# Cross-attention of a six-layer decoder kernel: context held once in float32 on four row groups, and scores computed twice

## The reference

```
q = layernorm(x).reshape(N, Q, 16, 16);  k = v = ctx.reshape(N, 375, 16, 16)
energy = einsum('nqhd,nkhd->nhqk', q, k)
energy = where(mask == 0, -1e20, energy)
attn   = softmax(energy / sqrt(256), axis=-1)
out    = einsum('nhqk,nkhd->nqhd', attn, v).reshape(N, Q, 256)
x      = x + out @ W_out.T
```

## Time and profile before

| | |
|---|---|
| median of three runs | 1690.42 us |
| the profiled execution | 1694.06 us |
| its span, first to last instruction | 1692.0 us |
| granted TensorE clock, mean | 0.942 |
| busy: TensorE, VectorE, ScalarE, GpSimd | 91%, 50%, 43%, 28% |
| phase A ends with VectorE's residual of its last batch | 360.1 us |
| phase B ends with its last residual | 685.5 us |

### The profile page before, as it was taken

How to read it: one execution, slowest core, us unless ns; L and a number is a source line. 1 busy time by engine, 2 the same in 40 slices (tenths; PEclk the granted TensorE clock), 3 DMA queues, 4 the chain that set the end, 5 groups by cost and what they waited for, 6 DMA issues and landing times.

```text
span 1692.0 us, 32657 instructions
## 1 busy us (share of the span) xinstructions
PE 1534.2 (91%) x10944; PEld 1093.8 (65%) x10944; DVE 840.0 (50%) x1896; ACT 731.2 (43%) x2003; POOL 480.1 (28%) x535
## 2 busy tenths in 40 slices
PE   5999999979888898599997999999989998899995
PEld 5888888857777787255554475656566665566553
DVE  2555555546666685355553121111136664566665
ACT  1111121126676686266664323122226664454552
POOL 1111111121111120598884000000023332455541
PEclk8999999977898898799998999999999999899995
DMA  8152221148797989000000100000000000000001
GB/s 202 48 93 65 64 62 55 55 72 102 105 108 92 107 101 207 1 1 0 0 1 1 47 1 1 0 0 0 0 6 1 0 0 1 9 9 11 8 4 44
DMA packets 58226, 71.10 MB, mean 42 GB/s; under 512 B 9552, under 2 KB 54848, under 8 KB 58160
## 3 DMA queue, kind: packets, MB, share of 16 engines
q1 hardware_dynamic: 58160, 70.23, 23.7%
HBM read 56.07 MB, written 14.15 MB: 41 GB/s over the span
## 4 chain that ended last, share of the span: by engine, by line
PE 76%; DVE 7%; DMA 6%; issue 4%; ACT 3%; POOL 2%; SPq 2%; DVEq 0%; ACTq 0%; POOLq 0%
PE banks L287 42%; PE banks L661 6%; DMA b_cp<-mask_scratch 5%; PE banks L280 4%; PE banks L566 3%; PE banks L597 3%; PE banks L674 3%; PE banks L687 3%; PE banks L587 2%; PE banks L613 2%; PE banks L538 2%; PE banks L664 2%; DVE area L1403 1%; PE banks L644 1%; DMA room<-in_bo 1%
## 5 line engine op out<-in xcount | busy, mean ns | idle before, releaser
L1109 ACT ACTIVATE area<-banks,area 112x112 f32<-112x112 f32 x768 | 208.9, 361 | 145.5 <-DVE area L1403 134.0
L661 PE MATMUL banks<-area 128*112 128x448 f32 x384 | 178.6, 547 | 7.7 <-ACT area L1109 3.9
L1349 DVE TENSOR_REDUCE area<-banks 112x2 f32<-112x750 f32 x128 | 119.9, 937 | 98.6 <-PE banks L587 97.6
L1403 DVE TENSOR_REDUCE area<-banks 112x4 f32<-112x448 f32 x192 | 119.4, 622 | 93.2 <-PE banks L664 92.9
L280 PE MATMUL banks<-cst,area 112*128 112x112 f32 x576 | 98.4, 287 | 72.4 <-DVE area L1446 21.6
L280 PEld LDWEIGHTS banks<-cst,area 112*128 112x128 f32 x576 | 62.8, 149 | 113.2 <-issue 81.9
L1076 ACT ACTIVATE room<-banks,area 112x375 f32<-112x375 f32 x256 | 132.6, 573 | 3.6 <-DVE area L1349 2.7
L287 PE MATMUL banks<-area,room 128*128 128x112 f32 x1024 | 124.9, 285 | 7.9 <-DVE area L1270 5.3
L287 PEld LDWEIGHTS banks<-area,room 128*128 128x128 f32 x1024 | 122.8, 202 | 8.4 <-DVE area L1270 5.5
L674 PEld LDWEIGHTS banks<-cst,area 112*112 112x112 f32 x768 | 87.5, 133 | 55.6 <-issue 44.1
L954 POOL TENSOR_TENSOR area<-area,cst 128x896 f32<-128x896 f32 x64 | 107.0, 1694 | 57.0 <-ACT area L1129 57.0
(11 more groups left out here) (205 smaller groups left out, 2888.8 us busy)
## 6 DMA issues: line engine op xcount, KB each, us to landing
b_cp<-parts_scratch SPq DMA_DIRECT2D x64, 375.0 KB, 12.5
parts_scratch<-Y_room SPq DMA_DIRECT2D x32, 375.0 KB, 3.8
Y_room<-in_ctxT SPq DMA_DIRECT2D x16, 375.0 KB, 4.5
Y_room<-in_ctx SPq DMA_DIRECT2D x16, 375.0 KB
l<-in_l SPq DMA_DIRECT2D x2, 1024.0 KB, 12.7
room<-in_ctxT SPq DMA_DIRECT2D x16, 112.0 KB, 2.1
out<-X SPq DMA_DIRECT2D x16, 112.0 KB, 1.8
X<-in_x SPq DMA_DIRECT2D x1, 1568.0 KB, 22.4
```

The costliest lines, as they stand in the source:

```text
L661: T3.matmul(pb[2 + g % 2][0:S, 0:4 * S], c_qT[u][:, k, :], c_kbd[u][:, k, j:j + 4, :].rearrange("p j s -> p (j s)"), start=True, stop=False)
L1109: last = a_.activation(c_p[:, h * S:(h + 1) * S], pb[2 + g % 2][0:S, j * S:(j + 1) * S], ACT.Exp, bias=c_nb[:, h:h + 1])
L1349: v_.tensor_reduce(b_nb[:, 2 * p:2 * p + 2], pair, AX_X, ALU.max, negate=True).then_inc(Bs["nb"].sem, 1)
L1403: v_.tensor_reduce(c_nb[:, 4 * g:4 * g + 4], pb[2 + g % 2][0:S, 0:4 * S].rearrange("q (j s) -> q j s", j=4), AX_X, ALU.max, negate=True).t ...
```

## The change

The high and low parts go away, with their making in phase A and with `parts_scratch`. The context is held once, as float32, and so are the queries. Each has 16 rows for a head and the heads lie at partitions 0, 32, 64 and 96 (`SLOT` = 32): four heads side by side, four such sets (`QUAD`) in the free dimension. Beside the 16 rows stand a row of ones in the context (against a row of the queries that is zero at first and later takes the negated maximum) and a row with the mask. There are four buffers of the context, `b_ctx`, and four of the queries, `b_q`.

The scores with queries on the partitions (`scores_b`) are computed as before but in float32, four heads on four row groups, and serve only the maximum. The 16 maxima of each query (`b_nb`) are transposed, copied by ScalarE into `b_nt` and written by a DMA into the four rows of `b_q`. Then a second product (`turned`) computes the scores again with the keys on the partitions, two heads at a time on two row groups, with the maximum subtracted by the extra row. Its result goes through one exponential of 125 by 896 straight to `b_pT`, with the mask as the bias. The 48 transposes of a batch and their 16 copies go away. The pieces of a batch are spread over four bodies; `by_four` writes 5 bodies out, loops twice over 4 and writes 7 out.

```diff
-        b_cp ... [STACK, H * SCP] F32R x2;  b_qs ... [STACK, H * S] F32R x2
+        b_ctx = [take(P, QUAD * SCP, "p (k s) -> p k s", k=QUAD) for _ in range(4)]
...
@@ sync
-                for c in range(4):
-                    src = parts_scratch[c % 2, bass.ds(b, 1)].rearrange("o (h r) s -> (o r) h s", r=HD)
-                    sp.dma_start(b_cf[u][HD * c:HD * c + HD, :, 0:SC], src).then_inc(Bs[f"cp{u}"].sem, 16)
+                for r in range(4):
+                    src = T["ctxT"][bass.ds(b, 1)].rearrange("o (a k c i) s -> a c (o i) k s", a=2, k=QUAD, c=2)[r // 2, r % 2]
+                    sp.dma_start(b_ctx[w][SLOT * r:SLOT * r + HD, :, 0:SC], src).then_inc(cp, 16)
...
+            for n in range(2):
+                values(n, n)
+            sp.wait_ge(pre["bx"].sem, 1)
+            for n in range(4):
+                context(n, n)
+            def ctx_loads(b, w, quarter):
+                if on(b - 1):
+                    sp.wait_ge(Bs["me"].sem, Bs["me"].at(b))
+                    sp.dma_start(b_q[(w - 1) % 4][HD:P:SLOT, :].rearrange("r (k s) -> r k s", k=QUAD),
+                                 b_nt).then_inc(Bs["mr"].sem, 16)
+                if on(b + 2) and on(b - 2):
+                    sp.wait_ge(Bs["st"].sem, Bs["st"].at(6 * (b - 1)))
+                    context(b + 2, (w + 2) % 4)
+                if on(b + 1) and on(b - 1):
+                    sp.wait_ge(Bs["vr"].sem, Bs["vr"].at(b))
+                    values(b + 1, (w + 1) % 2)
@@ tensor: the order of phase_b(b)
+                weighted(b - 2, 0);  scores_b(b, 0)
+                T3.transpose(pb[7][0:H, 0:S], b_nb[(w - 1) % 2], ident[0:S, 0:S])     # after nb(8b), nm(b-2)
+                turned(b - 2, 4);  weighted(b - 2, 1);  transposes(b_o) of b - 3
+                turned(b - 2, 5);  scores_b(b, 1);  products with wx0 of b - 3
+                turned(b - 1, 0);  4 transposes of b_xs, 128 columns each, for b + 1   # after xn, xu(b-2)
+                scores_b(b, 2);  turned(b - 1, 1);  weighted(b - 2, 2);  weighted(b - 2, 3)
+                turned(b - 1, 2);  scores_b(b, 3);  4 transposes of b_u of b - 2
+                turned(b - 1, 3)
+            def scores_b(b, k, w, quarter):
+                if k == 0:
+                    pe.wait_ge(Bs[f"cp{w}"].sem, Bs[f"cp{w}"].at(16 * 5 * (quarter + 1)))
+                    pe.wait_ge(Bs["qs"].sem, Bs["qs"].at(b + 1))
+                for r in range(4):
+                    if r % 2 == 0:
+                        pe.wait_ge(Bs["nb"].sem, Bs["nb"].at(8 * b + 2 * k - 1 + r // 2))
+                    o = SLOT * r
+                    last = T3.matmul(pb[r][0:S, 0:SC], b_q[w][o:o + HD + 2, k * S:(k + 1) * S],
+                                     b_ctx[w][o:o + HD + 2, k, 0:SC], start=True, stop=True)
+            def turned(b, n, w):
+                g, c = divmod(n, NKC)
+                if n == 0:
+                    pe.wait_ge(Bs["mr"].sem, Bs["mr"].at(16 * (b + 1)))
+                pe.wait_ge(Bs["ex"].sem, Bs["ex"].at(6 * b + n))
+                for k in range(QUAD):
+                    for e in range(2):
+                        o = SLOT * (2 * g + e)
+                        last = T3.matmul(pb[4 + e][0:KC, k * S:(k + 1) * S], b_ctx[w][o:o + HD + 1, k, c * KC:(c + 1) * KC],
+                                         b_q[w][o:o + HD + 1, k * S:(k + 1) * S], start=True, stop=True)
@@ scalar: the order of phase_b(b)
+                b_nt <- pb[7];  weights(b - 2, 4);  b_oT;  weights(b - 2, 5);  weights(b - 1, 0);  b_q for b + 1
+                weights(b - 1, 1);  b_u of b - 2;  weights(b - 1, 2);  weights(b - 1, 3)
+            def weights(b, n, v):
+                a_.activation(b_pT[g][:, c, :, :], banks[0:KC, 4:6, 0:QN], ACT.Exp, bias=b_bias[v][:, c:c + 1])
@@ vector: phase A loses line 1322; the order of phase_b(b)
+                normalise b - 3;  highest 0, 1;  layer norm of b + 1 into b_xs (two, 128 columns each);  highest 2
+                residual of b - 3;  highest 3, 4, 5;  stats of b + 2;  highest 6, 7
+            def highest(b, n, u):    # 112 x 750, two banks
+                dve.wait_ge(Bs["sg"].sem, Bs["sg"].at(4 * b + k + 1))
```

More of the change, by code:

```diff
@@ L123, in batches, with by_four @@
         body(b, b % 2, b // 2)
+def by_four(eng, body, ahead, behind):
+    for b in range(-ahead, 4):
+        body(b, b % 4, b // 4)
+    with eng.Fori(1, 3) as i:
+        for w in range(4):
+            body(4 * i + w, w, i)
+    for b in range(12, B + behind):
+        body(b, b % 4, b // 4)
 def decoder_kernel(nc, T, out):
@@ L306, in decoder_kernel @@
         top[0] = 0
[L307 to L313, removed]
         b_u = take(P, 4 * S)
@@ L316, in decoder_kernel, with beside_y @@
         b_oT = take(P, KT * S)
[L317 to L329, removed]
+        b_pT = [take(KC, 2 * NKC * QN, "p (c e n) -> p c e n", c=NKC, e=2) for _ in range(2)]
+        b_q = [take(P, QN) for _ in range(2)]
+        assert top[0] <= B_OWN
+        top[0] = B_OWN
+        b_ctx = [take(P, QUAD * SCP, "p (k s) -> p k s", k=QUAD) for _ in range(4)]
+        b_cv = [take(KC, NKC * H * 17, "p (c h e) -> p c h e", c=NKC, h=H)]
+        low = [0]
+        def beside_y(parts, n, pattern=None, **dims):
+            a = Y_room[0:parts, low[0]:low[0] + n]
+            low[0] += n
+            assert low[0] <= B * D
+            return a.rearrange(pattern, **dims) if pattern else a
+        b_in = [beside_y(KC, NKC * D, "p (c n) -> p c n", c=NKC) for _ in range(2)]
+        b_cv.append(beside_y(KC, NKC * H * 17, "p (c h e) -> p c h e", c=NKC, h=H))
+        b_xs = beside_y(S, H * SLOT)
+        b_mt = beside_y(KC, B * NKC)
+        b_bias = [beside_y(KC, NKC) for _ in range(2)]
+        b_nb, b_rc, b_nt = [beside_y(S, H) for _ in range(2)], beside_y(S, H), beside_y(H, S)
+        b_q = [beside_y(P, QN) for _ in range(2)] + b_q
         top[0] = 0
@@ L419, in part_stores @@
[L419 to L432, removed]
@@ new lines, in scores_b @@
+            def scores_b(b, k, w, quarter):
+                if k == 0:
+                    pe.wait_ge(Bs[f"cp{w}"].sem, Bs[f"cp{w}"].at(16 * 5 * (quarter + 1)))
+                    pe.wait_ge(Bs["qs"].sem, Bs["qs"].at(b + 1))
+                for r in range(4):
+                    if r % 2 == 0:
+                        pe.wait_ge(Bs["nb"].sem, Bs["nb"].at(8 * b + 2 * k - 1 + r // 2))
+                    o = SLOT * r
+                    last = T3.matmul(pb[r][0:S, 0:SC], b_q[w][o:o + HD + 2, k * S:(k + 1) * S], b_ctx[w][o:o + HD + 2, k, 0:SC],
+                                     start=True, stop=True)
+                last.then_inc(Bs["sg"].sem, 1)
@@ new lines, in weighted @@
+            def weighted(b, t, v):
+                g = t // 2
+                pe.wait_ge(Bs["ex"].sem, Bs["ex"].at(6 * b + 3 * (g + 1)))
+                if t == 0:
+                    pe.wait_ge(Bs["ue"].sem, Bs["ue"].at(b))
+                    pe.wait_ge(Bs["vr"].sem, Bs["vr"].at(b + 1))
+                    if isinstance(b, int) and b == 0:
+                        pe.wait_ge(pre["b6"].sem, 1)
+                for c in range(NKC):
+                    for j in range(4):
+                        n = 2 * (t % 2) + j // 2
+                        last = T3.matmul(pb[6][32 * j:32 * j + 17, t * S:(t + 1) * S], b_cv[v][:, c, 4 * t + j, :],
+                                         b_pT[g][:, c, j % 2, n * S:(n + 1) * S], start=(c == 0), stop=(c == NKC - 1),
+                                         tile_position=(0, 32 * j))
+                if t % 2:
+                    last.then_inc(Bs["pv"].sem, 1)
@@ L647, in _ @@
             pe.wait_ge(A["xu"].sem, A["xu"].at(B))
-            batches(pe, phase_b, 1)
+            for c in range(NKC):
+                last = T3.transpose(pb[7][0:KC, c * B:(c + 1) * B], mask_f[:, c * KC:(c + 1) * KC], ident[0:B, 0:B])
+            last.then_inc(Bs["kt"].sem, 1)
+            by_four(pe, phase_b, 1, 3)
             def attention(s, mask, project_qk, project_v, qk_read, to_columns, w_out, dst_out, col_g=2):
@@ new lines, in phase_b @@
+                if on(b):
+                    highest(b, 0, u)
+                    highest(b, 1, u)
+                if on(b + 1):
+                    dve.wait_ge(Bs["pc"].sem, Bs["pc"].at(2 * b + 4))
+                    dve.wait_ge(Bs["xq"].sem, Bs["xq"].at(b + 1))
+                    if isinstance(b, int) and b == -1:
+                        dve.wait_ge(pre["bx"].sem, 3)
+                    for a in range(2):
+                        dst = b_xs.rearrange("s (k a c e) -> s a k c e", k=QUAD, a=2, c=2)[:, a, :, :, 0:HD]
+                        src = xb_(b + 1, a * P, (a + 1) * P).rearrange("s (k c e) -> s k c e", k=QUAD, c=2)
+                        last = v_.tensor_scalar(dst, src, mv[:, 0:1], rstd[:, 1:2], ALU.subtract, ALU.mult)
+                    last.then_inc(Bs["xn"].sem, 1)
@@ new lines, in phase_b @@
+                if on(b):
+                    highest(b, 2, u)
+                if on(b - 3):
```

(7 more changed lines are left out.)

337 lines of the change are left out of this document (140 added, 197 removed).

## The result

The changed kernel takes 1815.88 us (median of 4 runs, 1815.43 to 1818.96), the kernel before 1690.66 beside it: ratio 1.074, interval 1.0679 to 1.08. It is slower by 125 us where I forecast 60 faster. The profiled execution took 1815.63 us.

A forecast was written before the change was run, and what follows sets the result against it. Phase A was taken as TensorE-bound, phase B as losing about 45 us to context waits. Phase B: 4.2 + 11 + 14 + 208.6 + 23.5 + 4 = 265.3, 60.1 less than 325.4, giving 1630 us, range 1608 to 1678.

The forecast's parts named there:

- the waits added: Phase B: waits the new order brings for exponentials, maxima and the maximum's DMA; 0.7 us of stall a body, the rest hidden.
- that wait disappears and the clock stays up: Phase B: the context, requested 1.6 bodies ahead at a quarter of the bytes, no longer delays TensorE; body 14.9 us.
- TensorE's sum at full clock: New body of phase B: TensorE's products sum to 14.2 us, plus 0.7 us of stall gives 14.9.
- The first rival: Phase B's products: fewer row groups run at once; pairs only adds 40 us, 1670 us, chance 0.11.
- the other estimate of the prediction, 0.82: Scores for the maximum: a set takes 0.82 us by the skill's 3.07 times, whole kernel 6 us longer than forecast.
- The rival of the round trip: Phase B: the maximum's way back by DMA becomes the bound; at 12.5 us, 121 longer, 1751 us; chance 0.08.
- Start: Start of phase B: first scores 4.2 us after phase A ends; then body 0 takes 11 us, body 1 14.
- Late instructions: Phase B code run for the first time breaks off mid-group; as a rival 42 us more, 1672 us, chance 0.08.
- What the wait for the context was worth: Old phase B: about 45 us lost over 15 bodies; rival that it stays: 1675 us, chance 0.03.
- The rest: Outside phase B: phase A still 20.42 us a body, its removals worth nothing; later phases unchanged in length.
- 4 us for late code: Phase B's sum: allowance for instructions arriving late, 4 us as before, bounds 0 to 40.

## Why the prediction was wrong

The step that failed is in "the waits added": "that wait disappears and the clock stays up". I took it for granted that a TensorE without gaps has its full clock, and worked every term of the sum at 0.43 us for 512 columns. The wait did disappear, and the clock went down for good. The same body at 14.66 us with 32 rows and at 26.66 with 17 and 18 puts 12.0 us a body on that step. The rows of the kernel before suggested the belief: there each of the seven falls of the clock between 406.65 and 685.50 stands beside a stop of TensorE of 2.2 to 6.8 us. They didn't show the reverse, that without stops there is no fall. And the earlier trace rows I misread: in the ninth and the seventeenth slice the clock is at 7 tenths with DMA at 4 and 0, not at 7 to 9.

- TensorE's sum at full clock, 14.2 + 0.7 = 14.9: right, 14.64 to 14.66 measured. Four row groups run at once and `turned` runs in pairs. The first rival, fewer groups at once, falls for the full bodies. A set takes 0.83 rather than 0.72 (the other estimate of the prediction, 0.82, was the better one), a pair of weighted sums 1.27 rather than 1.40. All changes of tiling mode are in these 14.66 us; no run takes one alone.
- Waits: right. At full clock one exponential of 1.02 us stands in the chain of a body (I had 0.7 us), no maximum and no DMA. The 2.3 and 4.0 us above are from the lower clock, where waits hide more easily. The rival of the round trip falls.
- Start, right at 4.15 us. Body 0 takes 13.2 us for my 11 and body 1 18.3 for 14, from first scores to first scores (365.82, 379.02, 397.30), and the low clock goes on through the bodies after them.
- Late instructions: mis-placed. Not new code but the branch back of a loop of four bodies stops, for 1.8 to 3.2 us. With 32 rows the stop and its dip make two bodies 16.3 us longer (22.81 + 22.79 - 2 x 14.66).
- What the wait for the context was worth: near, but with help. The 49 us for my 45 hold both stops of the earlier trace rows, which the sum counts once more with its 4 us for late code; the wait alone is some 39.
- The rest: phase A unchanged, the phases after within 1 us.

What my sum describes is the written-out kernel with 32 rows and filled start, at 1641.61 for 1630. Its phase B takes 268.9 us for my 265.3, and not by luck alone: from the first scores of body 2 to the end it is 232.2 for 208.6 + 23.5, body 1 takes 21.8 for 14, and the 4 us for late code aren't needed. Among the rivals there was none for the clock. No row ahead of the prediction has products on so few rows, and that should have been the reason to bound it: at 1.2 GHz the same sum gives 28.4 us a body, 16 x 13.5 = 216 more, 1846 us. The Trainium skill's TensorE: Matmul & The Clock Gate, section Part 1, says that the clock is set by how busy the engine has been, and its advice is to leave no long gaps. This case's trace disagrees in that sense of busy: 26.67 of 26.67 us busy at 0.50, with records back to back.

Not settled: where between 24 and 28 rows the change lies and what it depends on besides rows, since columns, kind of product and filling were not varied one by one. Nor what sets the length of a low stretch, which was 51.2 us at the start with 32 rows in the loop and 68.3 with 32 rows written out. Nor why the second low stretch of the filled kernels lasts 20.5 us twice.

## What to carry to other kernels

Before products are packed into row groups with a short contraction, look for a stretch in a trace with as few rows in use, and read its granted clock; a sum at 2.4 GHz can be off by a factor of two on an engine that never waits. Where the clock is at 0.5 and the engine is without gaps, first widen the products to rows that are there anyway (zeros against ones): it costs no instruction and here gave back 152 us. A loop whose body is long may stop at its branch back: the stops of 2.8 to 3.2 us cost 8.5 us with 28 rows, 16.3 with 32, 24.0 with only `turned` at 32 and 44.2 with only the scores at 32, most of it through the clock.

## What the runs showed of the hardware that was not expected

- The granted clock was 0.50 for 436.9 us, in which TensorE was busy for 427.0, with 34 and 72 of 128 rows in use in its two main products. The same with 48 and 96 rows (1813.71 us); with 56 and 112 rows 1665.84.
- The rows 18 to 31 that were added meet zeros on one side and ones on the other, so their products are all zero, and the clock rose with them (only in `turned` a row with the mask, row 17, came in besides). Whether it would rise with zeros on both sides, no run shows.
- Four float32 products with 18 rows each on four row groups took 1.54 us at 0.50 and, with 32 rows, 0.83 at 1.00, for eight records of 375 columns.
- The loop of four bodies stopped TensorE for 1.8 to 3.2 us at its branch back in all eight kernels that have it; written out, the same code ran without a stop in all four.
